# A transformer block on one core: the first loads in another order, and the attention stacks in 64-row blocks, two heads under one another

## What is computed

```
qkv  = x @ qkv_w.T + qkv_b               # 16 heads of 8 channels
attn = softmax(q @ k.T * 8 ** -0.5) @ v  # per batch and head, 512 x 512
x1   = layernorm(x + (attn @ fc_w.T + fc_b + x))
h    = silu(x1 @ w1.T * s1) * (x1 @ w2.T * s2)      # hidden 512, ternary weights
h    = gelu(h @ h1.T * s)
h    = gelu(h @ h2.T * s)
out  = layernorm(x1 + h @ w3.T * s3)
```

## Time and profile before

| what | value |
|---|---|
| median of 3 runs | 379.07 us (378.65 to 379.9) |
| the profiled execution, its own time | 380.18 us |
| span of the profiled execution | 378.4 us |
| busy in the span: PE, DVE, ACT, POOL | 330.8, 246.0, 246.9, 155.8 us |
| PE weight loads | 152.8 us |
| granted clock of PE, mean | 0.956 |

### The profile page before, as it was taken

The page is one execution under the profiler, slowest core; times in us unless marked ns, Lnnn a source line. Parts: engine busy times, 40 slices in busy tenths (PEclk is TensorE's granted clock), DMA queues, the critical chain, the costliest instruction groups (busy, mean ns, idle before and its releaser), DMA issues.

```text
span 378.4 us, 5154 instructions
## 1 busy us (share of the span) xinstructions
PE 330.8 (87%) x1625; PEld 152.8 (40%) x1650; DVE 246.0 (65%) x482; ACT 246.9 (65%) x427; POOL 155.8 (41%) x231
## 2 busy tenths in 40 slices
PE   5267879999999999999999989989989996968981
PEld 3164212222334443434444524535634441446750
DVE  4416877787778987777788787658678401044763
ACT  3314675676767787768976887676688788664320
POOL 9045992000004476000881456625389607017101
PEclk9778899999999999999999999999999998987996
DMA  4944200211221121202102302030000100000001
GB/s 99 276 123 98 33 28 3 43 23 21 45 36 38 29 39 19 35 11 42 31 0 37 49 2 44 11 61 14 17 2 1 29 3 0 1 2 0 6 23 31
DMA packets 21903, 13.29 MB, mean 35 GB/s; under 512 B 6771, under 2 KB 20723, under 8 KB 21875
## 3 DMA queue, kind: packets, MB, share of 16 engines
q1 hardware_dynamic: 21427, 12.53, 16.0%
q10 hardware_dynamic: 448, 0.39, 0.4%
HBM read 5.38 MB, written 1.05 MB: 17 GB/s over the span
## 4 chain that ended last, share of the span: by engine, by line
PE 67%; issue 8%; ACT 7%; DVE 6%; POOL 5%; SPq 4%; ACTq 2%; DMA 1%; POOLq 0%; DVEq 0%
PE f_bank L413 16%; PE pv_bank L453 16%; PE s_bank L426 13%; PE st_bank L437 12%; DVE negmax L757 3%; ACT prob L619 3%; PE f_bank L396 2%; SPq L379 2%; ACTq L331 2%; POOL hT L933 2%; ACT L619 1%; ACT h_nat L685 1%; PE st_bank L413 1%; PE f_bank L474 1%; DMA x_in<-in_L_attn_x_dram 1%
## 5 line engine op out<-in xcount | busy, mean ns | idle before, releaser
L757 DVE TENSOR_REDUCE negmax<-s_bank 128x1 f32<-128x512 f32 x256 | 167.3, 683 | 53.5 <-PE s_bank L426 52.5
L619 ACT ACTIVATE prob<-st_bank 128x512 f32<-128x512 f32 x256 | 141.4, 596 | 43.1 <-PE st_bank L437 32.1
L426 PE MATMUL s_bank<-stack 125*128 125x512 bf16 x256 | 93.3, 389 | 9.7 <-DVE negmax L757 5.5
L437 PE MATMUL st_bank<-stack 128*128 128x512 bf16 x231 | 83.6, 386 | 5.6 <-ACT prob L619 3.3
L453 PE MATMUL pv_bank<-prob,v_sb 128*32 128x512 f32 x512 | 73.0, 612 | 0.8 <-ACT prob L619 0.5
L413 PE MATMUL f_bank<-act,hT 128*128 128x512 f32 x208 | 66.5, 437 | 0.8 <-DVE act L832 0.6
L426 PEld LDWEIGHTS s_bank<-stack 125*128 125x128 bf16 x256 | 23.4, 98 | 71.5 <-DVE negmax L757 44.1
L437 PEld LDWEIGHTS st_bank<-stack 128*128 128x128 bf16 x256 | 23.6, 97 | 57.1 <-ACT prob L619 38.0
L921 POOL CAST mparts<-negmax 128x16 bf16<-128x16 f32 (+1 forms) x17 | 3.3, 196 | 98.6 <-DVE negmax L757 98.5
L413 PEld LDWEIGHTS f_bank<-act,hT 128*128 128x128 f32 x208 | 38.9, 190 | 10.6 <-issue 1.1
L967 POOL TENSOR_TENSOR act<-h_nat,act 128x512 fp32r<-128x512 f32 x24 | 30.1, 1277 | 0.3
(11 more groups left out here) (156 smaller groups left out, 387.4 us busy)
## 6 DMA issues: line engine op xcount, KB each, us to landing
stack<-parts SPq DMA_DIRECT2D x120, 48.0 KB
x_in<-in_L_attn_x_dram SPq DMA_DIRECT2D x4, 256.0 KB, 2.9
h_nat<-in_L_ffn_h_w_dram SPq DMA_DIRECT2D x1, 1024.0 KB, 8.4
work<-in_L_ffn_h_w_dram SPq DMA_DIRECT2D x1, 1024.0 KB, 9.9
x_res<-in_L_attn_x_dram SPq DMA_DIRECT2D x4, 256.0 KB, 2.7
out_dram<-y SPq DMA_DIRECT2D x4, 256.0 KB, 2.3
work<-in_L_ffn_w_w_dram SPq DMA_DIRECT2D x2, 256.0 KB, 4.8
stack<-parts ACTq DMA_DIRECT2D x8, 48.0 KB
```

Source lines behind the costliest of these rows:

```text
L426: nc.tensor.matmul(s_bank[n % NS][:, :], stack[0][0:MROW, h, qt * P:(qt + 1) * P], stack[1][0:MROW, h, :], start=True, stop=True).then_inc ...
L437: last = nc.tensor.matmul(st_bank[n % NST][:, to:to + nq], stack[1][:, h, kt * P:(kt + 1) * P], stack[0][:, h, q0:q0 + nq], start=True, st ...
L619: nc.scalar.activation(prob[:, n % NP, :], st_bank[n % NST][:, :], ACT.Exp, scale=SCALE).then_inc(ev_st, 1)
L757: nc.vector.tensor_reduce(negmax[:, g % 2, col:col + 1], s_bank[n % NS][:, :], AX.X, ALU.max, negate=True).then_inc(ev_s, 1)
```

## The change

1. **Stacks.** The tile becomes `[128, 8, 512]`: head h stands in the 64 rows from 64 * (h % 2), at place h // 2. Its 48 part rows are followed by 13 rows of zeros or ones, and 3 of maxima. S is 61 rows deep, T 64. The tables put the two heads of a pair next to one another in S (even, odd, even, odd for each query tile), and T goes through the heads of a group in turn as before, which also alternates between the halves.
2. `mrow` is two DMAs (one for each half) in place of one; the memsets of the stacks at the start are half as wide.
3. **Loads.** The step `more` is cut up: `lw` (w1, w2), `lh` (h1, then h2), `l3` (w3) are steps of their own, and x of batch 1 is loaded ahead of them; h2 stands after 12 of the spreads, `more` (fc_b and the scales) after the first three groups of maxima.
4. The transpose of the fc weights (`wf`) is moved ahead of the first q on PE, into another bank; the staging tiles of the FFN weights are four.
5. All five orders are written anew. `h_out` and the names `LT`, `TU` only re-index the same steps (TU is 1).

```diff
-more xin xres xin zq*2 zk*4 zq*6 mrow*2 xin mrow spread mrow spread mrow spread mrow spread mrow xres spread mrow spread mrow spread mrow spread xres
+xin lw lh xin zq*6 lh zq*2 zk*2 mrow zk*2 l3 mrow xin mrow more spread mrow spread xres mrow spread mrow spread mrow xres spread mrow spread mrow
...
-    MROW = P - NPART
+    TR = 64
+    MROW = TR - NPART
+    HB = H // 2
...
-        S_TILES += [(g, h0 + c, t0 + t, c * nt + t if nt == NT else t * nh + c) for c in range(nh) for t in range(nt)]
+        S_TILES += [(g, h0 + 2 * c + e, t, e * nh * nt // 2 + c * nt + t) for c in range(nh // 2) for t in range(nt) for e in range(2)]
...
-        stack = [sb(f"stack{i}", [P, H, N], BF16) for i in range(2)]
+        stack = [sb(f"stack{i}", [P, HB, N], BF16) for i in range(2)]
...
-        w_raw = [m[:, :, :].rearrange("p t c -> p (t c)") for m in (x1[0], x1[1], res[1])]
+        w_raw = [m[:, :, :].rearrange("p t c -> p (t c)") for m in (x1[0], x1[1], res[1])] + [aT[:, :]]
...
-                eng.dma_start(stack[i][0:SR, h, :], parts[i][HD * h:HD * h + HD, :, :]).then_inc(rep0[p], 16)
+                eng.dma_start(stack[i][TR * (h % 2):TR * (h % 2) + SR, h // 2, :], parts[i][HD * h:HD * h + HD, :, :]).then_inc(rep0[p], 16)
...
-                    sp.dma_start(stack[0][MROW:P, h0:h0 + nh, t0 * P:(t0 + nt) * P],
-                                 mT[0:m_rows(n), 0:m_tiles(n) * P]).then_inc(mrow[n % NG], 16)
+                    rows = m_rows(n) // 2
+                    for e in range(2):
+                        sp.dma_start(stack[0][TR * e + MROW:TR * e + TR, h0 // 2:(h0 + nh) // 2, :],
+                                     mT[rows * e:rows * (e + 1), 0:P]).then_inc(mrow[n % NG], 16)
...
-                    nc.tensor.matmul(s_bank[n % NS][:, :], stack[0][0:MROW, h, qt * P:(qt + 1) * P],
-                                     stack[1][0:MROW, h, :], start=True, stop=True).then_inc(ps_s, 1)
+                    rows = slice(TR * (h % 2), TR * (h % 2) + MROW)
+                    nc.tensor.matmul(s_bank[n % NS][:, :], stack[0][rows, h // 2, qt * P:(qt + 1) * P],
+                                     stack[1][rows, h // 2, :], start=True, stop=True).then_inc(ps_s, 1)
...
-                        last = nc.tensor.matmul(st_bank[n % NST][:, to:to + nq], stack[1][:, h, kt * P:(kt + 1) * P],
-                                                stack[0][:, h, q0:q0 + nq], start=True, stop=True)
+                        rows = slice(TR * (h % 2), TR * (h % 2) + TR)
+                        last = nc.tensor.matmul(st_bank[n % NST][:, to:to + nq], stack[1][rows, h // 2, kt * P:(kt + 1) * P],
+                                                stack[0][rows, h // 2, q0:q0 + nq], start=True, stop=True)
...
-                    nc.tensor.transpose(s_bank[0][:, 3 * P:4 * P], fc_nat, ident[:, :]).then_inc(ps_wq, 1)
+                    nc.tensor.transpose(s_bank[1][:, 0:P], fc_nat, ident[:, :]).then_inc(ps_wq, 1)
```

More of the change, by code:

```diff
@@ L8 @@
 SP_ORDER = """
-more xin xres xin zq*2 zk*4 zq*6 mrow*2 xin mrow spread mrow spread mrow spread mrow spread mrow xres spread mrow spread mrow spread mrow spread xres
-mrow spread mrow spread mrow spread mrow spread out mrow xres mrow out mrow out*2
+xin lw lh xin zq*6 lh zq*2 zk*2 mrow zk*2 l3 mrow xin mrow more spread mrow spread xres mrow spread mrow spread mrow xres spread mrow spread mrow
+spread mrow spread mrow xres spread mrow spread mrow spread out mrow spread xres mrow*2 out mrow out*2
@@ L101, in post_ln_block_kernel @@
     UNITS = [(b, 0, NT) for b in range(B)]
-    LU = len(UNITS) - 1
-    CU = 3
+    CU, LT, TU = 3, LAST, len(UNITS) - LAST
     OGROUPS = [(b, GH * j, 0, NT) for b in range(B) for j in range(NG)]
-    UNIT_OG = [NG * u + NG - 1 for u in range(B)]
+    UNIT_OG = [NG * b + NG - 1 for b, _, _ in UNITS]
     S_TILES, S_AFTER, T_TILES, T_FIRST, T_WIDE, P_OF, P_LAST = [], [], [], [], [], [], []
     for g, (b, h0, nh, t0, nt, og) in enumerate(GROUPS):
-        S_TILES += [(g, h0 + c, t0 + t, c * nt + t if nt == NT else t * nh + c) for c in range(nh) for t in range(nt)]
+        S_TILES += [(g, h0 + 2 * c + e, t, e * nh * nt // 2 + c * nt + t) for c in range(nh // 2) for t in range(nt) for e in range(2)]
         S_AFTER.append(len(S_TILES))
@@ L430, in step @@
                     if n == T_FIRST[g]:
-                        pe.wait_ge(mrow[g % NG], 16 * (g // NG + 1))
+                        pe.wait_ge(mrow[g % NG], 16 * 2 * (g // NG + 1))
                     if n < NST:
@@ L535, in step @@
                     hi, lo = ((hi0_t, lo0_t), (hi_gt, lo_gt))[layer]
-                    pe.wait_ge((hi, lo)[halves[0]], kk + 1)
+                    pe.wait_ge((hi, lo)[halves[0]], NK * (u - LT) + kk + 1)
                     if len(halves) == 2:
-                        pe.wait_ge(lo, kk + 1)
+                        pe.wait_ge(lo, NK * (u - LT) + kk + 1)
                     for k in ks:
@@ L634, in _ @@
                     if n:
-                        act.wait_ge(mrow[(n - 1) % NG], 16 * ((n - 1) // NG + 1))
+                        act.wait_ge(mrow[(n - 1) % NG], 16 * 2 * ((n - 1) // NG + 1))
                     nc.scalar.activation(mT[0:m_rows(n), 0:m_tiles(n) * P], space("m", n)[:, :].bitcast(BF16)[0:m_rows(n), 0:m_tiles(n) * P], ACT.Copy).then_inc(emptied("m", n), 1)
@@ L675, in _ @@
                         else:
[L676 removed]
+                            act.wait_ge(*((lo_g, n) if u < LT else (lo_gt, NK * (u - LT + 1))))
                         wait(act, ps_w3T, before(u))
[L678 removed]
+                    nc.scalar.activation(raw[:, k, cols(u)], space(*h_first(u, layer, k))[:, 0:width(u)], ACT.Copy if u < LT else ACT.Gelu,
                                          scale=hs[:, 2 + layer, k:k + 1]).then_inc(emptied(*h_first(u, layer, k)), 1)
@@ L915, in _ @@
                     nm, left = negmax[:, n % 2, 0:w], mres[:, 0:w]
-                    if tt > 1:
-                        nm, left = (a.rearrange("p (t h) -> p t h", t=tt) for a in (nm, left))
-                        hi, mid, lo = (mparts[:, :].rearrange("p (t m h) -> p t m h", t=tt, m=NPART)[:, :, i, :] for i in range(NPART))
-                    else:
-                        hi, mid, lo = (mparts[:, i * w:(i + 1) * w] for i in range(NPART))
+                    nm, left = (a.rearrange("p (e c) -> p e c", e=2) for a in (nm, left))
+                    hi, mid, lo = (mparts[:, 0:NPART * w].rearrange("p (e m c) -> p e m c", e=2, m=NPART)[:, :, i, :] for i in range(NPART))
                     nc.gpsimd.tensor_copy(hi, nm).then_inc(m_step, 1)
```

119 lines of the change are left out of this document (63 added, 56 removed).

## The result

The changed kernel is slower: 392.19 us (390.28 to 393.7, 4 runs) against 379.32, a ratio of 1.032 (1.030 to 1.035). The profiled execution has a span of 388.3 us, 9.9 over the one before. The forecast was 370 with a range of 348 to 392. Some executions of the experiments run more than 1.5% over the fastest one of the same kernel, at a lower granted clock; they are left out of the differences.

The account below looks back on a forecast made before the run. PE was taken as the bound, 97% busy at full clock from 54 to 300 us. Start -7, attention -8, FFN +5 and end +1 gave -9: profiled execution 380.18 to 371 us, median 370, range 348 to 392.

Parts of the forecast that it names:

- The start: Up to the first S: x of batch 1 issued earlier, so its transpose and the spreads come earlier; -7 us (-9 to -5).
- the shift is kept: From the start to the end: the start's -7 us carries through, since PE is the bound behind it with the same work.
- A pair saves 0.19: Scores on PE: a second score in the other half costs 0.01 to 0.03, not 0.22 us; 206 pairs counted.
- a change of shape costs 0.115 each way and 0.09 for an exposed load: PE, between 64-row scores and 128-row work: price in us per change, plus weights no longer loaded ahead.
- Rival 2: Scores and 128-row work on PE: changes of rows are free, only pairs count; 342 us, held back to 345 to 358; chance 0.25.
- Attention alone: Stretch without FFN: PE saves 9.8 us by pairs less changes, DVE lets most through; -8 us (-12 to 0).
- With the FFN: Stretch with FFN steps, PE the bound: pairs -20.9, changes +18.4, exposed loads +7.5; +5 us (-21 to +26).
- The end: Last stretch, with no S in it: pairs -1.3, changes +1.8, exposed loads +0.9; +1 us.
- The second DMA of mrow: SP, 0.77 us more on each of 17 writes, hidden in all but the shortest groups; 0 to +2, taken as 0.
- rival 1: Changes of shape on PE, mainly with the FFN, decide against it: 0.61 us a round trip, slower, 399 us; chance 0.30.
- from 0.42: Rival 1's threshold: us per round trip from which 88 of them eat the gains of pairs, attention and start.

Follow-up runs that it names:

- loads2: Kernel before with only the start's transfers cut up and reordered, h2 and w3 issued right behind h1: 376.84 us (before 379.68).
- loads3: As loads2, with h2 behind 8 spreads, w3 behind 20, and PE's first h2 transpose behind six S: 381.94 us (before 380.0).
- new_order_128: Changed kernel with its new orders and loads but without halves: each head in its own stack, scores 125 and 128 rows deep: 386.08 us (before 379.55).
- the three variants: new_order_128, new_order_low and the changed kernel, compared from the 128th to the 176th S at clock 1.00: 52.1, 60.4 and 53.4 us.
- old_order_96: Kernel before with scores 93 and 96 rows deep in place of 125 and 128: 383.92 us (before 379.68).
- halves_loads2: loads2 with the stacks in 64-row blocks and pairs of heads, on the old orders: 384.28 us, 7.4 over loads2.
- old_order_halves: Kernel before, its orders and loads kept, with 64-row stacks, pairs of heads and the two mrow DMAs: 391.18 us (before 379.55).
- old_order_low: Kernel before with only the scores' depth changed, to 61 and 64 rows in the lower half: 424.45 us once, 471.78 to 473.66 three times.
- new_order_low: As new_order_128, but scores 61 and 64 rows deep, all heads in the lower half, no pairs: 430.3 us.

## Why the prediction was wrong

- **The start, -7:** the size was right, -6.4, the mechanism in part. PE waited for the fc weights until 9.02 us (9.1 was worked out), x was transposed at 13.57 (14.4), the first S came at 22.12 (21 to 22). But the fc weights don't set it: loads2 and loads3 have no such wait, and their first S stands at 22.02 and 21.75, behind 3.95 and 5.21 us for the transfers that fill the stacks. Nor did the width of the stacks count for nothing: new_order_128, with the same loads and memsets of full width, has its first S at 24.36. That "the shift is kept" was too simple: of the 5.7 us that the loads alone gave, less than half reached the last T. In loads2 1.7 us go in attention alone, where PE stands 2.24 us for ACT's copy of the transposed maxima, which it didn't before.
- **A pair saves 0.19, a change of shape costs 0.115 each way and 0.09 for an exposed load:** right in size: 0.20, and 0.14 on average; S over an FFN step to the next score takes 0.98 us (0.9 to 1.0). The drain of which the Trainium skill, TensorEngine Tiling (Array Packing), Key Properties, tells fits the price at 64 rows too: it is 0.14 us a change by the three variants, though no row shows a drain as such. Rival 2, free changes of rows, is refuted.
- **Attention alone, -8:** this step failed. I let "most" of PE's 9.8 us through, since DVE had waited 13.6 us for S. It got 1.3, of which the halves are 0.9. DVE still waited 12.0 us for S, and among PE's weight loads the longest wait is now that of T for ACT's exponential, 16.8 us where it was 4.4: with two banks, S and T stand behind P in PE's queue, P behind ACT's exponentials, and those waits don't shrink when S and T do. The pairs moved PE from 97% to 87% busy, into waits. At the clock of 1.00 the halves gave 2.8 us over two thirds of the stretch; in the first third, with 7.4 us more at 1.2 GHz, they cost 1.8, and the forecast had the clock at nothing. No run gave the scores more banks or moved P, so what would let the 9.8 us through isn't shown.
- **With the FFN, +5:** this failed too: it was +16.9, of which the halves are 9.1. The net of pairs and changes was right at full clock (53.4 against 52.1 us for 48 S); what was missing is the clock. old_order_96 shows that fewer rows alone lower it. With the 0.38 us per us of that run, an estimate, the 6.9 us more at 1.2 GHz of halves_loads2 over loads2 are 2.6 of the 9.1. The 17.1 us of old_order_halves over the kernel before are 6.5 of its 12.0. What is left, 6.5 and 5.5, is near the +5 of the forecast.
- **The orders, not priced at all:** I used them to count pairs and changes, and took the work's placing as equal: the term was put at nothing without a reason. They cost 6.5 us in this stretch and 1.1 at the end, and gain 2.1 in attention. Which placing does it is open. With 128 rows (new_order_128 against loads2) they gain 3.0 us in attention and lose 3.4 from the 112th to the 192nd S and 5.4 from there to the last T, with as much time at 1.2 GHz as loads2 there (10.2 us each), so the time at the lower clock doesn't explain it.
- **The end, +1:** it was +0.8, but by luck: the halves gave -0.5, the rest is orders.
- **The second DMA of mrow, 0:** right; no wait of PE names it in the changed kernel.
- **The rivals:** the sign was rival 1's. Its mechanism wasn't: the changes cost the price of the forecast, 0.28 a round trip, not 0.61. It named "from 0.42" as the point where they decide. With the 1.3 us that attention gave in place of 8, that point falls to (22 + 1.3 + 6.4) / 88 = 0.34, and 0.28 stays under it. By these prices pairs and changes alone would have left the kernel a little faster, and the orders and the clock made it slower; that is a sum of measured terms and of the estimate for the clock, no run by itself shows it.

What stays open: how much of the changed kernel's 17.1 us more at 1.2 GHz with the FFN is cost (6.5 us by the estimate of 0.38). No run held its clock up.

## What to carry to other kernels

Before pricing a saving on the busiest engine, ask for each instruction what it waits for: a matmul that waits for a bank isn't shortened by running beside another, and 97% busy can hold a chain of waits. Packing the array in halves wants long runs of packed matmuls; with full-depth steps between, each round trip costs 0.28 us against 0.20 a pair. Look at the granted clock by stretch too: here both fewer rows and another order lowered it. And a change with new loads, a new layout and new orders has to be taken apart: here the loads alone were the gain, and the rest ate it.

## What the runs showed of the hardware that was not expected

- Two scores in different row halves start together: 148 neighbours of the changed kernel are within 0.01 us of one another, where full-depth scores stand 0.22 us apart. The second is free if its bank is.
- 64-row scores one at a time can hold the granted clock at 0.50 over 74 us with PE busy throughout (old_order_low, three of four executions long), and the same scores run at 1.00 from 76.8 us on in new_order_low. 96-row scores lower its mean to 0.930 to 0.948, where 128-row scores in the same order have 0.948 to 0.968.
- A loss or a gain at the start isn't carried on evenly: +6.1 us stayed +6.1 for some 255 us, -5.7 became -2.6.
